# Decoder layer on one core: the self attention's query stack with each head and batch as 128 columns side by side

## The reference

```python
q = proj(Wq, bq)                       # (batch, head, query, d), d = 8
k = proj(Wk, bk)
idx = jnp.clip(pos[None, :] - pos[:, None], -MAX_REL, MAX_REL) + MAX_REL
rk2 = rel_k[idx]                       # (query, key, d)
attn1 = jnp.einsum('bhqd,bhkd->bhqk', q, k)
attn2 = jnp.einsum('bhqd,qkd->bhqk', q, rk2)
attn = jax.nn.softmax((attn1 + attn2) / scale, axis=-1)
```

## Time and profile before

| what | value |
|---|---|
| median of 3 runs | 453.44 us |
| the runs | 453.2, 453.44, 458.25 us |
| profiled execution, its own time | 452.45 us |
| profiled execution, its span from first to last instruction | 450.7 us |
| TensorE (matmul) busy | 383.9 us, 85% |
| VectorE busy | 302.7 us, 67% |
| ScalarE busy | 232.0 us, 51% |
| GpSimd busy | 79.3 us, 18% |

### The profile page before, as it was taken

How to read it: one execution, slowest core, us unless ns; L and a number is a source line. 1 busy time by engine, 2 the same in 40 slices (tenths; PEclk the granted TensorE clock), 3 DMA queues, 4 the chain that set the end, 5 groups by cost and what they waited for, 6 DMA issues and landing times.

```text
span 450.7 us, 11284 instructions
## 1 busy us (share of the span) xinstructions
PE 383.9 (85%) x4714; PEld 287.2 (64%) x4729; DVE 302.7 (67%) x630; ACT 232.0 (51%) x331; POOL 79.3 (18%) x90
## 2 busy tenths in 40 slices
PE   4566387957879999999997999999999998899992
PEld 2254145834566777777776967677787656566772
DVE  4318982588978678999783789977966366056334
ACT  2271066720379692239894933278954424844440
POOL 8910000110250111003140120024021102511001
PEclk9768579976999999999999999999999999999997
DMA  4637204720010640210141603101100110000100
GB/s 99 178 112 205 57 2 145 188 83 23 7 29 3 188 132 30 80 26 1 35 136 28 177 1 106 38 5 50 27 20 8 62 45 6 1 1 1 24 1 23
DMA packets 29420, 26.87 MB, mean 60 GB/s; under 512 B 12673, under 2 KB 27962, under 8 KB 28602
## 3 DMA queue, kind: packets, MB, share of 16 engines
q1 hardware_dynamic: 26042, 25.86, 20.7%
q10 hardware_dynamic: 3136, 0.27, 0.5%
q0 software_dynamic: 192, 0.03, 0.0%
HBM read 18.38 MB, written 7.35 MB: 57 GB/s over the span
## 4 chain that ended last, share of the span: by engine, by line
PE 61%; DVE 18%; DMA 7%; ACT 5%; issue 4%; SPq 3%; POOL 1%; POOLq 0%; another core or an unknown queue 0%; DVEq 0%; ACTq 0%
PE ps_f L721 13%; PE ps_f L710 12%; PE ps_s L543 8%; PE ps_f L569 5%; PE ps_f L577 4%; PE ps_s L632 3%; PE ps_f L522 3%; DMA QS<-parts_by_head 3%; PE ps_f L673 3%; DVE MX L946 3%; DVE ST L970 2%; PE ps_s L536 2%; DVE MX L942 2%; DVE ST L939 2%; PE ps_f L511 2%
## 5 line engine op out<-in xcount | busy, mean ns | idle before, releaser
L543 PE MATMUL ps_s<-QS,KS 125*128 125x128 bf16 (+1 forms) x768 | 78.8, 246 | 14.5 <-DVE ST L939 9.9
L543 PEld LDWEIGHTS ps_s<-QS,KS 125*128 125x128 bf16 (+1 forms) x768 | 63.3, 104 | 39.0 <-DVE ST L939 12.8
L842 ACT ACTIVATE HT<-ps_f,hb 128x512 f32<-128x512 f32 x72 | 48.4, 687 | 70.4 <-PE ps_f L710 34.8
L721 PEld LDWEIGHTS ps_f<-w,HT 128*128 128x128 f32 x576 | 69.0, 192 | 11.4 <-issue 5.4
L721 PE MATMUL ps_f<-w,HT 128*128 128x128 f32 x576 | 74.0, 279 | 0.1
L710 PE MATMUL ps_f<-x2T,w 128*128 128x512 f32 x144 | 71.2, 599 | 0.0
L484 POOL TENSOR_SCALAR_AFFINE_SELECT PC<-PC 128x1024 f32<-128x1024 f32 x32 | 34.8, 1093 | 150.7 <-ACT PC L806 150.7
L1054 DVE SCALAR_TENSOR_TENSOR acc<-ps_f,gw,acc 128x128 f32<-128x128 f32 x128 | 35.7, 340 | 23.8 <-PE ps_f L721 23.4
L799 ACT ACTIVATE ST<-ST 128x1024 f32<-128x1024 f32 x32 | 33.7, 1059 | 26.8 <-DVE ST L970 26.6
L939 DVE TENSOR_TENSOR ST<-ps_s,ST 128x1024 f32<-128x1024 f32 x32 | 38.5, 1202 | 11.5 <-PE ps_s L543 10.8
L806 ACT ACTIVATE PC<-ps_s 128x1024 f32<-128x1024 f32 x32 | 32.6, 1030 | 20.4 <-PE ps_s L543 16.6
(11 more groups left out here) (116 smaller groups left out, 528.6 us busy)
## 6 DMA issues: line engine op xcount, KB each, us to landing
parts_by_head<-part SPq DMA_DIRECT2D x16, 384.0 KB, 2.8
QS<-parts_by_head SPq DMA_DIRECT2D x24, 256.0 KB, 3.7
KS<-parts_by_head SPq DMA_DIRECT2D x24, 256.0 KB, 4.5
xin<-in_x SPq DMA_DIRECT2D x16, 64.0 KB, 2.4
cin<-in_ctx SPq DMA_DIRECT2D x4, 256.0 KB, 5.3
w<-in_L_ffn_rw SPq DMA_DIRECT2D x1, 1024.0 KB
out_x<-acc SPq DMA_DIRECT2D x16, 64.0 KB, 1.8
RV<-rel_v_by_distance SPq DMA_DIRECT2D x1, 512.0 KB, 3.8
```

What stands on the lines that cost most here:

```text
L543: last = nc.tensor.matmul(ps[:, o:o + S], KS[a][0:kd, c:c + S], queries(a, kd, h, j), start=not masked and j == 0, stop=j == NB - 1, skip_ ...
L721: last = nc.tensor.matmul(ps[:, b * E:(b + 1) * E], HT[n % 2][:, f, b * S:(b + 1) * S], w2[:, e, f, :], start=f == 0, stop=f == NF - 1 and ...
L842: nc.scalar.activation(HT[n % 2][:, f, :], ps[:, :], ACT.Gelu, bias=hb[:, e, f:f + 1]).then_inc(ht_ready, 1)
```

## The change

QS[0] gets the column order of QS[1]: (b q) within a head. The high part and the rest of q are written without turning the columns. p1 reads 128 columns side by side. bias reads, for its query, 64 single columns that lie 128 columns (256 bytes) apart, in the same order (head, batch) as before, so what it writes is unchanged. p2, the DMAs, the order of the steps and all waits are as before.

```diff
             def queries(a, kd, h, b):
-                if a:
-                    return QS[1][0:kd, (h * NB + b) * S:(h * NB + b + 1) * S]
-                return QS[0][0:kd, h * NB * S:(h + 1) * NB * S].rearrange("k (q b) -> k q b", b=NB)[:, :, b]
+                return QS[a][0:kd, (h * NB + b) * S:(h * NB + b + 1) * S]
...
-            qs_q = QS[0][0:KZ, :].rearrange("k (h q b) -> k h q b", h=H, q=S)
+            qs_q = QS[0][0:KZ, :].rearrange("k (c q) -> k c q", q=S)
...
                         last = nc.tensor.matmul(ps[:, j * HB:(j + 1) * HB], RK[0:KZ, S - 1 - q:2 * S - 1 - q],
-                                                qs_q[:, :, q, :], start=True, stop=True)
+                                                qs_q[:, :, q], start=True, stop=True)
...
                     hi, src = part[i][:, HIGH, :], ps[:, :]
-                    if what == "q":
-                        hi, src = hi.rearrange("p (q b) -> p q b", b=NB), src.rearrange("p (b q) -> p q b", b=NB)
                     nc.scalar.activation(hi, src, ACT.Identity, bias=bcol[:, b:b + 1]).then_inc(hi_ready[what], 1)
...
                     left, src, hi = rest[k][:, :], ps[:, :], part[i][:, HIGH, :]
-                    if what == "q":
-                        left, hi = (m.rearrange("p (q b) -> p q b", b=NB) for m in (left, hi))
-                        src = src.rearrange("p (b q) -> p q b", b=NB)
                     nc.vector.scalar_tensor_tensor(left, src, bcol[:, b:b + 1], hi,
                                                    ALU.add, ALU.subtract).then_inc(rest_ready[what], 1)
```

## The result

The changed kernel takes 499.56 us (median of 4 runs, 494.63 to 503.52) against 455.22 (median of 4, 453.2 to 458.25) of the kernel before in the same comparison: 1.0932 times, 95% interval 1.0808 to 1.1055. I had forecast slower, at 482, with 490 as the upper end. The direction held, the size did not.

A forecast was written before the change was run, and what follows sets the result against it. TensorE was taken as the bound, never idle around chunk 2's and 3's bias steps; +6.5 (chunk 0), +8.1 (chunk 1) and +14.4 (chunks 2 and 3) made +29.0 on 452.45 us, 481.5, stated as 482, range 452 to 490.

The forecast's parts named there:

- reading (a): Bias read: price per 16-byte stretch touched, 116 ns a matmul, the forecast's own choice; chance 0.66.
- reading (b): Rival on the bias read: price per 8 bytes, 59 ns a matmul, 454.5 us in all; chance 0.20.
- the free jump: Rival: only close spacings are slow, bias stays at 29.7 ns and p1's gain remains, 445 us; chance 0.06.
- the further latency: Rival: single columns show more latency, 230 ns a bias matmul, 540 us; chance 0.04.
- w2: Step touching 32 far-apart stretches, 62 ns for four records, taken as evidence on the bias read's price.
- Chunk 0: Slower bias steps let VectorE take up p1 at 41.6 us in place of 35.06, +6.5 us.
- 1.38 us a step: Each bias step of 16 matmuls goes from 0.475 to 1.86 us; 8 steps make +11.05 in chunks 2 and 3 each.
- Whatever a matmul gains or loses there moves the end one for one: Chunks 2 and 3: TensorE never idle around bias and p1 steps, so each change there counts in full.
- p1's 8.2 us: Gain from p1's side-by-side read: 7.7 us in chunks 2 and 3, 0.5 in chunk 1.
- a gain of 0.5: Chunk 1: the last three p1 steps, read side by side, give back 0.5 us in all.
- The other rival on p1: p1's slowness isn't its spacing, so p1 gains nothing and bias pays all the same, 490 us; chance 0.04.

The follow-up runs named there:

- sweep: Kernel before, each of the eight bias steps reading its 64 columns in a different spacing, values from other queries; run once, 473.62 us.
- busy_bias: Kernel before, bias steps lengthened by three full-rate matmuls of 512 adjacent columns ahead of each eight; 492.27 us, ratio 1.0819.
- p1_slow: Kernel before, p1 reading its 128 columns 16 bytes apart, bias as before; 476.99 against 454.83 us, ratio 1.0447.
- p1_again: Kernel before, only p1 reading side by side, bias as before, second measurement of that kernel; 452.21 against 454.83 us, ratio 0.993.
- pairs: Kernel before, bias reading pairs of columns and p1 fours, both 8 bytes at a time, values from other queries; 460.59 us, ratio 1.0135.

## Why the prediction was right or wrong

- **The price of the new read: right.** 116 ns by reading (a), 111 to 115 measured; reading (b), 59, is out, and so are the free jump and the further latency. What decided for (a) was w2, and the sweep bears it out. That row was thin ground, though: w2's 62 ns are 5 above what (a) gives it (57), as they are 8 above (b)'s.
- **Reads within 16 bytes: in part.** The Trainium skill, SBUF — State Buffer, section Specifications (TRN2), wants at least two reads in each 16-byte line for full bandwidth. The sweep agrees that reads within 16 bytes share the price, but two are not enough: two a line cost 57 to 59 ns for 64 columns, twice the 29 to 30 of four or eight a line. The same page's note on cachelines (in the section on the DMA port swizzle) has a spacing of 8 bf16 elements as free; it costs 115 ns here, and the measurement decides.
- **Chunk 0: right.** VectorE takes up line 932 (939 before) at 41.44 us; I had 41.6. The chunk grew by 6.6 us for my 6.5.
- **The bias steps at full clock: right.** busy_bias has 8.6, 10.3 and 10.4 us; at my price of 1.38 a step it would be 8.6, 11.05 and 11.05.
- **1.38 us a step as all that chunks 1 to 3 lose: wrong.** I priced the read and left the neighbours at the clock they had. The stretches around the slow reads were granted 0.69 to 0.77, and the transposes, projections and up steps between them went down to half rate. Against my terms that is 0.8, 4.3 and 3.7 us; against busy_bias, whose steps are as long as the real ones, 0.8, 5.1 and 4.4. Behind the stretches it took more (the sum, below).
- **"Whatever a matmul gains or loses there moves the end one for one": wrong for gains.** It is the step on which p1's 8.2 us rested. Measured on the changed kernel it is 0.4 us in the rest of chunk 2 and 1.4 behind chunk 3's bias steps for 3.9 each. TensorE without idle time only says that nothing else is late yet; how early the others are, does not show. Losses do count one for one, and more (p1_slow). In chunk 1, 3.4 us were lost behind the bias steps where I had a gain of 0.5: 1.5 between x1T and c1.0, at a granted 0.50, and 1.9 in the issue ahead of w2 (2.7 us for 0.8), which I did not isolate.
- **The sum.** 29.0 + 8.8 (clock and bias stretches: 9.4 + 15.4 + 14.7 less 8.6 + 11.05 + 11.05) + 3.5 + 2.5 (p1 in chunks 2 and 3) + 3.9 (behind chunk 1's) + 0.1 = 47.8, against 48.0 between the two spans. The last 9.9 us, behind the bias stretches, are not all p1's missing gain. The clock took 1.5 of them in chunk 1 and, by my estimate, up to 1.4 in chunk 2 (the two p1 steps 1.70 us for 0.92, the transposes 0.86 for 0.46, the four matmuls behind them 0.72 for 0.53); p1_again, whose clock did not fall there, lost 0.9 of the same gain to waits. The issue ahead of w2 took 1.9, which differs between executions. So the miss of 18.8 us splits roughly into 11.7 for the clock, 5.1 for p1's gain and 1.9 for that wait, each to a us or two.
- **The other rival on p1**, that its slowness isn't its spacing, gave 490 and for the wrong reason: p1 did become quick, but that brought 0 to 3 us of its 8.2.

What stays open: which share of p1's gain the instruction issue, VectorE and the transfers each take. With VectorE relieved and the transfer sooner the gain is still only some 2.4 us, and I have shown the waits at the places, not a kernel in which all of them are gone. And why the clock falls with reads at a quarter of the rate and not at half: the runs show that it does, not by what rule.

The clearly quicker versions all leave out three quarters of the maxima, which keep the exponential's argument small, so they are no replacement. Of the column orders tried, its own (four batches of a query together) is the best: it keeps bias at the clock's rate and lets p1 be slow where that is covered.

## What to carry to other kernels

When a layout makes one reader quick and another slow, count for each read how many of its elements share 16 bytes, price both, and then ask in which of the two TensorE's time is covered; here equal sums of TensorE time (pairs) differed by 1.35% of the whole. A busy share of 100% makes losses count, and promises nothing of gains: before a gain is booked, look how long the next things that TensorE will wait for have been done when it comes. And do not leave the clock where it was when a read becomes slow: look what stands between and behind the slow matmuls.

## What the hardware showed that I had not expected

- A TensorE filled with slow reads lost its clock. The stretch before held 1.00; with bias matmuls of 111 ns in it, 0.69 to 0.77, and the records show TensorE busy all the time (28.29 of 28.29 us). With the same length filled by reads at full rate it is 1.00, with reads at half rate (57 ns) too. With p1 at 227 ns a matmul (p1_slow) it is 0.92 in a stretch that had 1.00.
- The slow read's pace does not hang on the clock: a bias matmul takes 111 ns at a granted 0.50, and 110 (chunk 3) to 115 (sweep) at 1.00. p1's 8-byte read was at 1.09 us a step at both too, which says less: 128 columns side by side at 0.50 are 107 ns a matmul already.
- The moving operand costs 1.7 to 1.8 ns for each 16 bytes touched, near or far; from four bf16 columns in each on nothing shows of it.
